# Expert stage of an AdaLN block with a top-2 mixture of experts: the small row-weight and row-number copies go from VectorE to ScalarE and later in the tile, and the weight split on GpSimd is cut into pieces of 512 columns

## What is computed

```
x = hidden_states
out = _swiglu(x, shared_gate_up, shared_down)
probs = softmax(x @ gate_weight.T)
top_p, sel = top_k(probs, 2); top_p /= sum(top_p)
for e in range(8):
    y = _swiglu(x, experts_gate_up[e], experts_down[e])   # inner width 938
    out = out + cw[..., e:e + 1] * y                       # cw: top_p where e was chosen, else 0
```

## Time and profile before

| | us |
|---|---|
| time, median of 3 runs (lowest to highest) | 966.2 (965.87 to 968.27) |
| span of the profiled execution | 967.3 |
| PE busy | 740.5 |
| VectorE (DVE) busy | 678.6 |
| ScalarE (ACT) busy | 430.4 |
| GpSimd (POOL) busy | 395.5 |
| line 1468, 19 copies of 128x4 | 48.5 |
| lines 386 and 391, 8 instructions each on 128x3072 | 42.8 and 55.7 |
| line 1105, 188 of 128x512 | 162.7 |

### The profile page before, as it was taken

One profiled execution on the slowest core, in us unless ns is written; L12 is line 12 of the kernel. 1 busy time (PEld: TensorE's weight loads), 2 busy tenths in 40 slices (PEclk: granted clock), 3 DMA queues, 4 the chain that ended last, 5 costly groups with the idle time before them and its releaser, 6 DMA issues.

```text
span 967.3 us, 11710 instructions
## 1 busy us (share of the span) xinstructions
PE 740.5 (77%) x3134; PEld 555.3 (57%) x3135; DVE 678.6 (70%) x1358; ACT 430.4 (44%) x721; POOL 395.5 (41%) x299
## 2 busy tenths in 40 slices
PE   4556988879787888887766969696995977869940
PEld 1435756657565555565554747474874866657830
DVE  3576878787877879774637676767658677676637
ACT  2324564646465564732432525252542543435520
POOL 2231434535445444443325352626225344342136
PEclk9566798979898989978977979797997997979985
DMA  8210000000000001010322020201102102000017
GB/s 250 29 60 17 15 9 25 20 22 22 22 22 22 22 0 38 6 42 6 114 82 71 28 75 24 78 22 39 66 20 71 33 14 79 23 20 25 25 56 224
DMA packets 38204, 44.40 MB, mean 46 GB/s; under 512 B 5334, under 2 KB 28880, under 8 KB 38184
## 3 DMA queue, kind: packets, MB, share of 16 engines
q1 hardware_dynamic: 33576, 35.69, 12.1%
q0 software_dynamic: 4608, 8.47, 2.7%
HBM read 31.42 MB, written 13.76 MB: 47 GB/s over the span
## 4 chain that ended last, share of the span: by engine, by line
PE 48%; DVE 25%; issue 14%; POOL 5%; ACT 3%; DMA 2%; DVEq 0%; SPq 0%; ACTq 0%; POOLq 0%
PE PS L554 45%; DVE aux_w L1468 5%; PE PS L557 3%; DVE acc L1121 2%; DVE nx_a L1092 2%; DVE prod L1100 2%; POOL al L409 2%; DVE al L1105 2%; POOL sorted_dram L443 1%; POOL c_exp L424 1%; POOL rstd_b L418 1%; DVE yT L1205 1%; DVE nx_b L1092 1%; ACT xsT L915 1%; DMA stage<-result_dram 1%
## 5 line engine op out<-in xcount | busy, mean ns | idle before, releaser
L1100 DVE TENSOR_TENSOR prod<-PS,sg 128x512 f32<-128x512 f32 x216 | 149.0, 690 | 145.8 <-PE PS L554 130.3
L884 ACT CAST ah<-prod 128x512 fp32r<-128x512 f32 x216 | 132.9, 615 | 204.1 <-DVE prod L1100 204.1
L554 PE MATMUL PS<-xh,w_lo 128*128 128x512 f32 x432 | 188.2, 436 | 29.2 <-DVE prod L1100 17.0
L513 POOL DMA_INDIRECT result_dram<-y_rows,aux_d x80 | 91.3, 1142 | 272.4 <-DVE y_rows L1451 238.1
L879 ACT ACTIVATE sg<-PS 128x512 f32<-128x512 f32 x216 | 129.2, 598 | 154.8 <-PE PS L554 154.4
L554 PE MATMUL PS<-xh,w_hi 128*128 128x512 f32 x432 | 177.8, 412 | 0.0
L554 PE MATMUL PS<-xl,w_hi 128*128 128x512 f32 x432 | 177.8, 411 | 0.0
L1105 DVE TENSOR_TENSOR al<-prod,ah 128x512 fp32r<-128x512 f32 x188 | 162.7, 865 | 12.1 <-ACT ah L884 10.3
L554 PE MATMUL PS<-al,w_hi 128*128 128x512 f32 x216 | 96.8, 448 | 74.4 <-DVE al L1105 67.5
L554 PEld LDWEIGHTS PS<-xh,w_lo 128*128 128x128 f32 x432 | 87.6, 203 | 60.8 <-DVE prod L1100 25.2
L443 POOL DMA_INDIRECT sorted_dram<-h,slot x64 | 69.9, 1092 | 101.6 <-DVE slot L1291 73.1
(11 more groups left out here) (215 smaller groups left out, 1120.2 us busy)
## 6 DMA issues: line engine op xcount, KB each, us to landing
stage<-in_w_gu SPq DMA_DIRECT2D x18, 469.0 KB
xin<-sorted_dram SPq DMA_DIRECT2D x20, 260.0 KB, 2.7
stage<-in_w_dn SPq DMA_DIRECT2D x9, 448.0 KB
tab<-mods_dram SPq DMA_DIRECT2D x8, 384.0 KB, 3.4
sorted_dram<-pad SPq DMA_DIRECT2D x8, 260.0 KB, 2.6
out<-X SPq DMA_DIRECT2D x4, 512.0 KB, 3.2
stage<-result_dram SPq DMA_DIRECT2D x3, 512.0 KB, 5.2
result_dram<-y_rows,aux_d POOLq DMA_INDIRECT x80, 2.3
```

The source lines that it names most:

```text
L513: pool.indirect_dma_start(out=result_dram, out_offset=bass.IndirectOffsetOnAxis(ap=aux_d[:, 0, r:r + 1].bitcast(U32), axis=0), in_=y_rows[ ...
L554: return nc.tensor.matmul(out, lhsT, rhs, start=start, stop=stop, **k)
L884: A.copy(ah[:, c % 3, :], prod[:, c % 3, :]).then_inc(s["ah_ready"], 1)
L1100: V.tensor_tensor(prod[:, c % 3, :], bank("up", where, c), sg[:, c % 3, :], ALU.mult).then_inc(s["prod_done"], 1)
```

## The change

Three edits. (1) `take_tile` on VectorE keeps only the subtraction that gives `xl`; ScalarE copies weight and row number together into a new tile `aux_next` in `split_tile`, and from there to `aux_w` and `aux_d` in `move_aux`, at c = 6 (`FC - 2`), behind `high(6)` and ahead of `high(7)`. The row number is a float until this last copy turns it into an integer. `give_rows` waits for the copy. (2) `split_expert` does the split in 6 pieces of 512 columns, the low part of a piece one piece behind the high part. (3) Semaphores follow.

```diff
-        token2 = sb("token2", [P, CH, 2], I32)
+        token2 = sb("token2", [P, CH, 2])
...
-        aux_w = sb("aux_w", [P, 2, TR])
-        aux_d = sb("aux_d", [P, 2, TR], I32)
+        aux_next = sb("aux_next", [P, TR, 2])
+        aux_w = sb("aux_w", [P, TR])
+        aux_d = sb("aux_d", [P, TR], I32)
...
+        PIECES = 6
...
+            def split_expert(x, buf):
+
+                pool.wait_ge(s["raw_in"], 16 * NRAW * (x + 1))
+                apart(pool)
+                n = WC // PIECES
+                for k in range(PIECES + 1):
+                    if k < PIECES:
+                        at = slice(k * n, (k + 1) * n)
+                        V.tensor_tensor(w_hi[buf][:, at], stage[:, at], M["ones"][:, 0:1].to_broadcast([P, n]),
+                                        ALU.mult).then_inc(s["cut_hi"], 1)
+                    if k:
+                        at = slice((k - 1) * n, k * n)
+                        pool.wait_ge(s["cut_hi"], PIECES * (x - 2) + k)
+                        last = V.tensor_tensor(w_lo[buf][:, at], stage[:, at], w_hi[buf][:, at].bitcast(F32),
+                                               ALU.subtract)
+                last.then_inc(s["split_done"], 1)
...
                     pool.wait_ge(s["y_bank_done"], SHARED + first)
-                    split_hi(e + 2, 1 - buf)
-                    split_lo(e + 2, 1 - buf)
+                    split_expert(e + 2, 1 - buf)
...
             def split_tile(i):
                 act.wait_ge(s["xt_done"], i + 1)
                 A.copy(xh[:], PS[:, 7, :]).then_inc(s["rh_ready"], 1)
+                act.wait_ge(s["aux_moved"], i + 1)
+                A.copy(aux_next[:], xin[:, :, P:P + 2]).then_inc(s["aux_read"], 1)
+
+            def move_aux(i):
+
+                act.wait_ge(s["results_out"], 64 * (i + 1))
+                act.wait_ge(s["aux_read"], i + 2)
+                A.copy(aux_w[:], aux_next[:, :, 0])
+                A.copy(aux_d[:], aux_next[:, :, 1]).then_inc(s["aux_moved"], 1)
...
                         high(SHARED + i, c)
+                        if c == FC - 2:
+                            move_aux(i)
...
-            def take_tile(i, moved):
+            def take_tile(i):
 
                 dve.wait_ge(s["rh_ready"], i + 1)
                 V.tensor_tensor(xl[:], PS[:, 7, :], xh[:].bitcast(F32), ALU.subtract).then_inc(s["rl_ready"], 1)
-                if moved:
-                    dve.wait_ge(s["aux_moved"], i)
-                V.tensor_copy(aux_w[:, 1, :], xin[:, :, P])
-                V.tensor_copy(aux_d[:, 1, :], xin[:, :, P + 1].bitcast(I32)).then_inc(s["aux_read"], 1)
...
             def give_rows(i):
 
                 dve.wait_ge(s["yt_done"], SHARED + 1 + i)
+                dve.wait_ge(s["aux_moved"], i + 1)
...
                         low(SHARED + i, c)
-                        if c == FC - 3:
-                            dve.wait_ge(s["results_out"], 64 * (i + 1))
-                            dve.wait_ge(s["aux_read"], i + 2)
-                            V.tensor_copy(aux_w[:, 0, :], aux_w[:, 1, :])
-                            V.tensor_copy(aux_d[:, 0, :], aux_d[:, 1, :]).then_inc(s["aux_moved"], 1)
-                    take_tile(i + 1, True)
+                    take_tile(i + 1)
```

More of the change, by code:

```diff
@@ L95, in constants @@
     return (np.ascontiguousarray(big, np.float32), np.ascontiguousarray(small, np.float32),
-            np.ascontiguousarray(token, np.int32))
+            np.ascontiguousarray(token, np.float32))
 SMALL = {}
@@ L242, in adaln_block @@
             xh_ready xl_ready logits_done lg_ready soft_in soft_out picked_ready counts_done counts_read
-            rows_ready sorted_out dve_chain raw_in split_hi split_done piece_hi piece_done gate_done up_done silu_done prod_done
+            rows_ready sorted_out dve_chain raw_in split_hi split_done cut_hi piece_hi piece_done gate_done up_done silu_done prod_done
             ah_ready al_ready al_late y_bank_done y_sb_ready yt_done y_out gated_free tile_in xt_done rh_ready
@@ L458, in _ @@
             pool.wait_ge(s["setup_mem"], 1)
-            V.memset(pad[:, :, P + 1:P + 2].bitcast(I32), NOWHERE).then_inc(s["setup_mem"], 1)
+            V.memset(pad[:, :, P + 1:P + 2], float(NOWHERE)).then_inc(s["setup_mem"], 1)
             pool.wait_ge(s["setup_mem"], 2)
@@ L500, in _ @@
             apart(pool)
-            pool.sem_inc(s["split_hi"], 1)
             pool.sem_inc(s["split_done"], 1)
@@ L514, in results @@
                         out=result_dram, out_offset=bass.IndirectOffsetOnAxis(
-                            ap=aux_d[:, 0, r:r + 1].bitcast(U32), axis=0),
+                            ap=aux_d[:, r:r + 1].bitcast(U32), axis=0),
                         in_=y_rows[:, r, :], in_offset=None, bounds_check=2 * TOKENS - 1,
@@ L1285, in place @@
                     V.tensor_tensor(h2[:, k, :, P], top[:, 4 + k, :], top[:, 7, :], ALU.mult)
-                    V.tensor_copy(h2[:, k, :, P + 1].bitcast(I32),
+                    V.tensor_copy(h2[:, k, :, P + 1],
                                   token2[:, bass.ds(g * GC, GC), k:k + 1].rearrange("p j o -> p (j o)"))
@@ L1333, in _ @@
             V.memset(aux_w[:], 0.0)
-            link(V.memset(aux_d[:], NOWHERE))
+            V.memset(aux_d[:], NOWHERE).then_inc(s["aux_moved"], 1)
             dve.wait_ge(s["setup_mem"], 2)
@@ L1434, in _ @@
             gate_shared(g, WIDE)
-            def take_tile(i, moved):
+            def take_tile(i):
                 dve.wait_ge(s["rh_ready"], i + 1)
                 V.tensor_tensor(xl[:], PS[:, 7, :], xh[:].bitcast(F32), ALU.subtract).then_inc(s["rl_ready"], 1)
-                if moved:
-                    dve.wait_ge(s["aux_moved"], i)
-                V.tensor_copy(aux_w[:, 1, :], xin[:, :, P])
-                V.tensor_copy(aux_d[:, 1, :], xin[:, :, P + 1].bitcast(I32)).then_inc(s["aux_read"], 1)
             dve.wait_ge(s["plan_ready"], 1)
-            take_tile(0, False)
+            take_tile(0)
             def give_rows(i):
                 dve.wait_ge(s["yt_done"], SHARED + 1 + i)
+                dve.wait_ge(s["aux_moved"], i + 1)
                 V.tensor_tensor(y_rows[:], PS[:, 7, :].rearrange("p (r d) -> p r d", r=TR),
-                                bc(aux_w[:, 0, :].unsqueeze(2), [P, TR, P]), ALU.mult).then_inc(s["y_out"], 1)
+                                bc(aux_w[:].unsqueeze(2), [P, TR, P]), ALU.mult).then_inc(s["y_out"], 1)
             with dve.Fori(0, E) as e:
```

## The result

The changed kernel takes 979.16 us (median of 4 runs, 977.72 to 979.37), the kernel before 967.23 beside it (4 runs, 965.87 to 968.27). The ratio is 1.0127, 95% interval [1.0105, 1.0149]: **slower by 1.3%**, where 909 us were predicted. It is the time of the rival with 4%, *the pieces don't let go*.

A forecast was written before the change was run, and what follows sets the result against it. The prediction took GpSimd's long split instructions, which hold VectorE and so TensorE, as what the change could relieve: 967.3 - 85.8 + 2 + 14 + 11 + 2 = 910.5 as profiled, 909 us as median, range 890 to 937.

The forecast's parts named there:

- the pieces don't let go: Rival at piece boundaries: GpSimd keeps VectorE out through all twelve, `al` waits 14.0 us, time 979 us; chance 0.04.
- What bounds the kernel now: Expert stage: GpSimd's long split instructions hold VectorE's `al` and small copy, which get in when one ends; 85.8 us.
- the stall: Seven tiles with a weight split are 85.8 us too long in all, everything that the change can win.
- the short waits: During the split, `al` waits for single pieces, costing TensorE 2.0 us per split: +14 us, bounds 7 and 64.
- what is late next: Tile behind a split: scatters and the `xin` load each come 1.6 us late, side by side: +11 us, bounds 0 and 28.
- the clock: TensorE's matmuls behind idle stretches run partly at a lower clock in one or two splits: +2 us, bounds 0 and 11.
- The copies: Small copies moved from VectorE to ScalarE: almost nothing gained by the move, +2 us for ScalarE's, bounds 0 and 12.
- What would show it: Profile signs: `al` up to about 2.0 us, tiles with a split 19 to 21 us; wrong if `al` lasts over 3.

The follow-up runs named there:

- e1: Changed kernel with each of the twelve pieces waiting for the one before it, low part right behind its high part: 923.47 us, ratio 0.9547.
- e12: e1 with `xin` loaded ahead of the next weights, and ScalarE's scatter wait and small copies moved behind the copy to `xh`: 888.64 us, ratio 0.9192.
- e9: Changed kernel with a single wait behind the first of the twelve pieces: 912.64 us, ratio 0.9443.
- e16: Changed kernel with first and last piece of 256 columns, the others of 512, no pause: 967.86 us, ratio 1.002.
- e18: Changed kernel with eight pieces of 384 columns, no pause: 980.96 us, ratio 1.0156.
- e15: Changed kernel with twelve pieces of 256 columns, no pause: 923.47 us, ratio 0.9569.
- e17: Changed kernel with a first piece of 512 columns and ten of 256, no pause: 920.73 us, ratio 0.952.
- e8: Changed kernel with a single wait in the middle, behind the sixth of the twelve pieces: 924.36 us, ratio 0.9564.
- e13: The load and copy reorderings of e12 with the single wait of e9: 889.87 us, ratio 0.9226.
- e19: e18 with one wait behind the first piece: 923.81 us, ratio 0.9568.

## Why the prediction was wrong

**The step that failed** is in "What bounds the kernel now": "when it ends the one that waited gets in", and in the rival: "Against it stands the `al` that got in between `w_hi` and `w_lo`". The row was read rightly and carried too far. The two instructions of the earlier trace rows depend on each other: `w_lo` waits by a semaphore for `w_hi`, and it starts at 513.38, 0.08 behind the end of `w_hi` at 513.30. The `al` got in through this pause. The change puts a piece between each high part and its low part, so that no wait is left to be served: it removes the pause as it makes the pieces. The diff and the order of the instructions showed that; I counted the pieces and not the pauses. The same reading made and the earlier trace rows look like support, though neither shows an `al` waiting at a boundary without a pause.

The Trainium skill's page "SBUF — State Buffer", section "Who interferes with whom", says that the order of issue decides who is blocked. The trace disagrees where instructions follow without a pause: the `al` that it starts at 507.55 stood ahead of eleven pieces by their starts (508.04 and later) and went behind them all.

**The terms of the sum**, with the runs in which the pauses are there:

- **-85.8, the stall.** The mechanism and the size were right, for another kernel: 80.0 came back in e1's seven tiles, 77.8 in e12's.
- **+14, the short waits.** Oversized: what is left in e1's seven tiles is 5.8, and TensorE's waits for `al` are 3.7 in all. An `al` was held up to 1.0 us longer than alone, and TensorE felt 0.5 of it at most at once: the slack took more than I gave it. In e9 the term comes out as forecast: its seven tiles are 137.9 - 124.5 = 13.4 above seven times 17.79.
- **+11, what is late next.** Right in place and in kind; in e9 the waits are 8.1 + 3.2 = 11.3 us. For e1 it was undersized: 25.5 us (16.2 for `xin` in 4 splits, 9.3 for `ah` in 3), 3.6 for each instead of 1.6. For `xin` it comes from both ends: from the tile's start at 494.24 the load landed at 529.76, 35.5 in (34.0 predicted; the split ended at 27.6 rather than 26.7, and the load took 5.27 rather than 4.76), and the tile was 18.55 long, not 19.8, so that TensorE wanted it at 31.7 rather than 32.4. A difference of two large times, each a little off, gave 3.9 for 1.6. The bound above, 4 each, held for the mean but not for every tile (4.5 at most).
- **+2, the clock.** Undersized: in the four tiles of e1's second windows the granted clock is 0.86 to 0.93, and TensorE is busy for 20.0 us each where an ordinary tile has 17.8, 9 us in four tiles. In all seven tiles behind a split it is busy 17.5 us longer than before, at 0.81 to 0.93 where they had 1.00.
- **The copies.** ScalarE's cost 0, not 2. "Almost nothing gained" by the move was 5 us beside whole instructions, and nothing that can be told beside pieces.

So the same sum, for e1: 910.5 - 8.2 (short waits: 80.0 came back, not 71.8) - 2 (copies) + 24.3 (what is late and the clock: the twelve tiles without a split took 222.5 by their transposes' starts and take 259.8, 37.3 more and not 13) - 3.3 (the stage begins at 494.24 rather than 497.59, for a reason that stays open) = 921.3, its span. The time of 923.5 lies in the predicted range, but that is luck in part: errors of opposite sign stand behind it. e9, which is the change and one pause, is the kernel that the sum describes best: 967.3 - 85.8 + 13.4 + 19.3 (the twelve other tiles, 241.8 for 222.5; 13 forecast) - 4.6 (the stage begins at 493.03) = 909.6, its span, where the sum had 910.5. Without the earlier start, which no term foresaw, it would be 914.

**The rival that came.** Its place, its price and its sign were right: 979 against 979.16. It had `al` wait 14.0 rather than 12.4; the trace has 13.38, since `al` comes 0.51 into the split. Seven times 1.6 was 11.2; the windows show 9.2, and 0.8 elsewhere. Its chance of 0.04 was the fault. One row spoke against it, of a boundary of another kind than the ones that it was about, and the prediction took the page on SBUF to decide nothing there. Without a row of the kind in question it was a bet of even chances or so, and the range should have reached to 979.

**What would show it** worked: "wrong if `al` still lasts over 3 us" was seen at once.

## What to carry to other kernels

Cutting a long GpSimd instruction into pieces is not enough to free VectorE: pieces of 512 and 384 columns kept it out to the end, and pieces of 256 let it in within 2.5 us, but no longer when most pieces were of 512 (e16). A pause between them freed it every time. Give GpSimd a wait on its own last instruction behind the first piece, or behind each (0.08 us each), and look in the trace whether the waiting instruction still spans several pieces. A row supports a claim only if it is of the same kind as the case: an instruction that gets in between two others says nothing of two that follow without waiting. And what lay hidden behind a stall (here a load and a scatter, 35 us) must be moved in the same change, or it takes nearly half of the gain back (44 us left of 79).

## What the runs showed of the hardware

- A VectorE instruction with two SBUF inputs was kept out by up to sixteen GpSimd instructions in a row, 14.5 us (e18), though each was only 0.8 to 1.0 us long. A pause of 0.08 us let it in each of 287 times.
- Without a pause it depends on the lengths of the pieces in a way that I can't state: 384 and 512 columns kept it out for the whole split; with 256 it got in ahead of every high part and of no low part (e15, e17: 80 of 80 and 0 of 53), but in e16, where pieces of 512 stand between them, it was the other way round (0 of 7 and 14 of 14). Behind one pause, later boundaries without one were nearly all open too (127 of 132 in e8, e9, e13, e19).
- A product that reads one input from PSUM was never held: the longest in the expert stage is 0.694 us in e1, where products ran beside the pieces, and 0.694 in the changed kernel and in e18.
